# Four layers in 128 slots on one core: another timetable for the side work

## The chip, the cores and the metric

The kernel runs on one core of a Trainium2 chip. Its five engines work side by side, each through its own queue in order: PE (TensorE, matrix products and transposes), DVE (VectorE), ACT (ScalarE), POOL (GpSimd), and SP (SyncE), which here only issues DMAs. They wait for each other by semaphores. SBUF is the on-chip memory, PSUM the memory into which PE writes. The metric is the time of one execution on the device, in microseconds; a kernel's time is the median of its runs.

## The reference

An input x of 16 sequences, 512 tokens, 256 features goes through two layers, each an attention-like part and a feed-forward part, with a layer norm ahead and a residual around each. All of it is float32.

```python
x = x + _L0_attn_ref(_layernorm(x), ...)   # 16 heads, scores squared and masked, no softmax
x = x + _L0_ffn_ref(_layernorm(x), ...)    # silu(gate) * up, int8 weights, 768 hidden
x = x + _L1_attn_ref(_layernorm(x), ...)   # Mamba, forward and backward, 512 channels, 16 states
x = x + _L1_ffn_ref(_layernorm(x), ...)    # the same form, inputs and weights rounded to fp4 blocks

def step(h, ins):                          # the Mamba recurrence, over 512 tokens
    dt_t, u_t, B_t, C_t = ins
    h = jnp.exp(dt_t[..., None] * A) * h + (dt_t * u_t)[..., None] * B_t[:, None, :]
    y_t = jnp.einsum('bdn,bn->bd', h, C_t)
    return (h, y_t)
```

## The kernel before

The Mamba recurrence is the backbone. For one sequence (a block, b) there are 2 directions x 16 states x 4 groups of 128 channels = 128 scans over 512 tokens. Each is a **slot**, j = 0 to 127, and every engine walks through the slots of a block and then through the next block; the loop body holds one whole block. In slot j the fixed work is:

- POOL: for even slots the product B x (dt u) for two groups of slot j+4 (inflow, L786, 128x1024); in every fourth slot the sum of the last two token tiles (add_last, L797).
- ACT: the decay exp(dt A) of slot j+2 into one of three PSUM banks (decay, L1017), and in half of the slots the weighing of a transposed state by C (weigh_last, L1025).
- DVE: scan j (L1296), and in half of the slots the sum of a weighed state into y (add_state, L1307).
- PE: the transposes of a finished state, six slots behind (turn_state, L1598, four per slot).
- SP: in every fourth slot the row of B for the state seven slots on.

Everything else, the **side work**, is put between these: the other three layers and the rest of Mamba, of the same sequence or of the one before or after. It is cut into pieces with names: a_ is the first layer's attention (a_score the scores, with ACT's squares; a_mask POOL's mask, L732; a_weigh and a_sums the weighting of the values and the division; a_onturn and a_wo the output), f_ its feed-forward, p_ and m_ the input side of Mamba (p_in projection, p_conv convolution, p_silu, p_x, p_dt the step sizes), z_in the gate, i_turn, d_turn, d_gate and d_out the output side, q_ the fp4 feed-forward (q_gate, q_silu, q_up; q_hquant and q_htail the rounding). Five layer norms per block are split into x_stat (moments on DVE, then a root on ACT, L843 to L845), x_norm on DVE (four instructions on 128x4 elements, L1137, L1139, L1141, L1143) and the scaling on ACT (L851); x is a, f, m (twice: norm2, norm3) and q. m_x (L760) is a residual on POOL behind the scaling of norm2.

A table of rows sets the slot of every step of every piece on every engine, an entry like 50 or 22.1. On one engine the steps of a slot come after its fixed work, in the order of these numbers, and steps with the same number in the order of the rows. The fraction only orders. PE's products of side work share three PSUM banks; which bank a step gets follows from PE's part of the table, and so does the step whose reader it waits for (take_bank). Everything else that a step waits for is named by the code and does not depend on the table. The steps of an engine wait in place: one that is early holds all behind it, the scans too.

For the sequences at the ends the loop is written out, with the steps of sequences that do not exist left out; about 240 us run before the first scan and 110 behind the last one.

## Time and profile before

| what | value |
|---|---|
| median of 3 runs | 6433.99 us |
| lowest and highest | 6428.44, 6437.33 us |
| the profiled execution | 6432.07 us, span 6430.3 us |
| DVE, POOL, PE, ACT busy | 75%, 73%, 71%, 65% of the span |
| TensorE clock granted, mean | 0.849 |
| DMA | 308.76 MB, 15% of the 16 DMA engines' time |

The profile is one execution, with each instruction's start and duration, and for the idle time ahead of one the instruction elsewhere that ended it. Block 7 of 0 to 15 is read as the example: its first scan starts at 2914.16 us, the next block's at 3299.95, 385.8 later; the blocks from 2 on lie within 3 us of that. In it slot 29 starts at 2991.54, slot 50 at 3050.56, slot 84 at 3150.13, slot 91 at 3169.78, slot 96 at 3190.07, slot 109 at 3238.71 and slot 112 at 3248.55 us, by the starts of DVE's scans.

### The profile page before, as it was taken

The numbers are of one execution on the slowest core, as the hardware profiler recorded it, in microseconds if no ns is written. First come the engines' busy times: TensorE is split into PE (matmuls) and PEld (weight loads), VectorE is DVE, ScalarE is ACT, GpSimd is POOL, SyncE is SP. The second block draws the span as 40 slices with busy tenths as digits, with TensorE's granted clock in tenths as the row PEclk, the third lists the DMA queues.
The fourth block names the chain that finished last, engine by engine and source line by source line (L and its number), as shares of the span: only waits on it lengthen the run. The fifth ranks groups of instructions, "written<-read, shape, count | busy, mean of one in ns | idle before, by whom it ended". The sixth has DMA issues, their size and how long they took to land.

```text
span 6430.3 us, 79973 instructions
## 1 busy us (share of the span) xinstructions
PE 4560.3 (71%) x21853; PEld 2957.7 (46%) x21900; DVE 4819.5 (75%) x6052; ACT 4188.8 (65%) x7079; POOL 4676.2 (73%) x2442
## 2 busy tenths in 40 slices
PE   6676677777777777677777777777677777777565
PEld 4344454444445444354444445444354444445443
DVE  5477786877878787786877878787786877868774
ACT  4566666666666666666666666666666666666563
POOL 1477777778776777777778776777777778776884
PEclk9787888888888888888888888888888888888777
DMA  3111111111111111111111111111111111111110
GB/s 118 38 43 45 43 55 37 57 44 39 60 37 57 39 58 45 43 54 38 57 44 39 60 37 57 39 58 45 43 57 31 60 44 40 60 37 52 35 47 29
DMA packets 152789, 308.76 MB, mean 48 GB/s; under 512 B 20870, under 2 KB 58310, under 8 KB 149926
## 3 DMA queue, kind: packets, MB, share of 16 engines
q1 hardware_dynamic: 152278, 302.80, 15.2%
q8 instruction: 217, 3.56, 0.2%
q14 instruction: 294, 2.41, 0.1%
HBM read 285.90 MB, written 16.84 MB: 47 GB/s over the span
## 4 chain that ended last, share of the span: by engine, by line
PE 39%; ACT 19%; DVE 19%; issue 16%; POOL 6%; DVEq 1%; ACTq 0%; POOLq 0%; DMA 0%; SPq 0%
PE psum L1598 8%; DVE arena_m L1296 6%; PE psum L1411 5%; PE psum L1579 4%; ACT psum L1017 4%; ACT hc L1025 3%; POOL arena_m L786 3%; PE psum L1524 3%; PE psum L1469 3%; PE psum L1487 3%; PE psum L1452 2%; PE psum L1423 2%; DVE arena_m L1307 2%; ACT arena_a L886 2%; ACT L837 2%
## 5 line engine op out<-in xcount | busy, mean ns | idle before, releaser
L786 POOL TENSOR_TENSOR arena_m<-bS,arena_m 128x1024 f32<-128x1024 f32 x1024 | 2409.1, 2365 | 325.9 <-PE psum L1598 325.7
L1296 DVE TENSOR_TENSOR_SCAN arena_m<-psum,arena_m 128x512 f32<-128x512 f32 x2048 | 2439.8, 1209 | 105.2 <-ACT psum L1017 51.1
L1598 PE MATMUL psum<-ident,arena_m 128*128 128x128 f32 x8192 | 1477.7, 319 | 994.2 <-ACT hc L1025 690.8
L1598 PEld LDWEIGHTS psum<-ident,arena_m 128*128 128x128 f32 x8192 | 1133.7, 165 | 1615.1 <-issue 814.6
L1017 ACT ACTIVATE psum<-arena_m,Aneg 128x512 f32<-128x512 f32 x2048 | 1406.2, 693 | 573.7 <-DVE arena_m L1296 569.6
L797 POOL TENSOR_TENSOR arena_m<-arena_m,hc 128x1024 f32<-128x1024 f32 x512 | 1217.0, 2377 | 292.2 <-ACT hc L1025 291.8
L1307 DVE SCALAR_TENSOR_TENSOR arena_m<-psum,Ct,arena_m 128x512 f32<-128x512 f32 x1024 | 754.1, 737 | 535.0 <-PE psum L1598 516.7
L1025 ACT ACTIVATE hc<-psum,Ct 128x512 f32<-128x512 f32 x1024 | 695.5, 679 | 43.3 <-PE psum L1598 43.1
L886 ACT ACTIVATE arena_a<-psum 128x512 f32<-128x512 f32 (+3 forms) x1024 | 380.8, 439 | 402.7 <-PE psum L1411 316.7
L1411 PE MATMUL psum<-arena_a 64*128 64x512 f32 (+3 forms) x2048 | 441.7, 533 | 252.8 <-ACT arena_a L886 108.7
L732 POOL TENSOR_SCALAR_AFFINE_SELECT arena_a<-arena_a 128x512 f32<-128x512 f32 x256 | 165.1, 655 | 445.5 <-ACT arena_a L886 445.5
L1487 PE MATMUL psum<-wB,arena_a 128*128 128x352 f32 x1024 | 408.4, 534 | 94.5 <-ACT arena_m L992 46.9
L1250 DVE SCALAR_TENSOR_TENSOR arena_m<-psum,convw,arena_m 128x509 f32<-128x509 f32 (+2 forms) x384 | 287.1, 748 | 168.6 <-ACT arena_m L948 159.4
L741 POOL TENSOR_TENSOR arena_a<-arena_a 128x704 f32<-128x704 f32 (+1 forms) x80 | 144.9, 1811 | 349.3 <-DVE arena_a L1084 349.3
L1411 PEld LDWEIGHTS psum<-arena_a 64*128 64x128 f32 x2048 | 192.6, 212 | 393.2 <-issue 150.8
L1452 PE MATMUL psum<-arena_a,wA 128*128 128x512 bf16 x1105 | 280.7, 399 | 83.7 <-DVE arena_a L1189 41.4
L1487 PEld LDWEIGHTS psum<-wB,arena_a 128*128 128x128 f32 x1024 | 207.9, 223 | 182.0 <-issue 90.8
L1524 PE MATMUL psum<-xnT,wU 128*128 128x512 f32 x512 | 275.4, 666 | 11.3 <-DVE arena_m L1250 8.4
L948 ACT ACTIVATE arena_m<-psum,convb,convw 128x512 f32<-128x512 f32 x128 | 99.5, 777 | 230.4 <-PE psum L1524 230.2
L1579 PE MATMUL psum<-wO,arena_m 128*128 128x256 f32 x1024 | 246.4, 387 | 4.0 <-DVE xF L1279 1.8
L1532 PE MATMUL psum<-xnT,wU 128*128 128x512 f32 x512 | 236.4, 594 | 0.0
L1357 PE MATMUL psum<-ident,arena_a 128*128 128x128 f32 x640 | 125.3, 344 | 136.8 <-ACT arena_a L851 118.6
(150 smaller groups left out, 7252.8 us busy)
## 6 DMA issues: line engine op xcount, KB each, us to landing
bS<-brow SPq DMA_DIRECT2D x512, 256.0 KB, 3.3
...
```

The source lines that it names most:

```text
L786: pool.tensor_tensor(hb[s % HBS][:, two, :], bS[:, s % 2, :].unsqueeze(1).to_broadcast([P, 2, T]), du[r][:, two, :], ALU.mult).then_inc(m_ ...
L797: pool.tensor_tensor(yT[:, 2:4, :], yT[:, 2:4, :], hc[:, s % 2, :, :], ALU.add).then_inc(m_yl.sem, 1)
L886: act.activation(asq[i][:, 2 * (j % 2) + j // 2, :], bank("a_score", None, w)[:, c:c + n], ACT.Square).then_inc(a_sq.sem, 1)
L1017: act.activation(EB[j % EBS], dt[r][:, m, :], ACT.Exp, scale=Aneg[:, r, m, n:n + 1]).then_inc(m_dA.sem, 1)
L1025: act.activation(hc[:, s % 2, i, :], HT[i], ACT.Copy, scale=Ct[:, r, 2 + i, n:n + 1]).then_inc(m_hc.sem, 1)
L1296: dve.tensor_tensor_scan(v, EB[j % EBS], v, 0.0, ALU.mult, ALU.add).then_inc(m_scan.sem, 1)
L1307: dve.scalar_tensor_tensor(yT[:, i, :], HT[i], Ct[:, r, i, n:n + 1], yT[:, i, :], ALU.mult, ALU.add).then_inc(m_y.sem, 1)
L1411: ins = pe.matmul(bank("a_score", None, w - 1 + half)[:, c:c + n], kT[rows, ht, i * P:(i + 1) * P], qm[rows, j, i * P:T], start=True, stop ...
L1487: ins = pe.matmul(bank(piece, None, w)[:, 0:FIH], xTq[:, k, i * P:(i + 1) * P], w_[:, k, c * FIH:(c + 1) * FIH], start=(k == 0), stop=(k = ...
L1524: ins = pe.matmul(bank("p_in", r, m), wU[:, k, m * P:(m + 1) * P], xnT[:, k, :], start=(k == 0), stop=(k == KD - 1))
L1579: ins = pe.matmul(bank("d_out", r, i // 2)[:, (i % 2) * D:(i % 2 + 1) * D], zs[:, m, i * P:(i + 1) * P], wO[:, m, :], start=(m == 0), stop ...
L1598: ins = pe.transpose(HT[i % 2][:, m * P:(m + 1) * P], hb[s % HBS][:, m, i * P:(i + 1) * P], ident[:, :])
```

## The change

Only the table changes: the numbers in nearly all of its rows, and the order of some rows. No operation, buffer or named wait is touched; which of the three banks a product gets, and so which reader it waits for there, is worked out anew from the new table. Its core:

```diff
-        row("a_mask", None, 1, POOL=[14, 17, 17, 19, 21, 25, 26, 26, 29, 32, 36, 37, 41, 45, 46, 46])
+        row("a_mask", None, 1, POOL=[10, 17, 17, 19, 19, 26, 28, 29, 39, 39, 40, 40, 44, 48, 48, 48])
-        row("q_norm", None, -1, ACT=[65], DVE=[50])
+        row("q_norm", None, -1, ACT=[67], DVE=[29])
...
-        row("m_x", None, 1, POOL=[86])
+        row("m_x", None, 1, POOL=[89])
...
-        row("p_silu", 0, 1, ACT=[107])
+        row("p_silu", 0, 1, ACT=[108])
```

Other entries that matter below, before and after: m_norm2 on DVE 86 and 87; m_norm3 on ACT 94 and 91.4; f_norm on DVE 59 and 58, its root on ACT 58 and 58; a_sums 3 on DVE 50 and 52; a_onturn on PE 52 and 53, on ACT 52.1, 52.2 and 52, 52; p_dt of direction 1 on POOL 39, 39, 43, 53 and 40, 43, 47, 52; d_out of direction 0 on PE 75, 77, 81, 81 and 74, 76, 77, 78; the first q_gate on PE 87 and 89; p_in of direction 0 on PE from 96 and from 95; the last q_gate on ACT 108 and 110 and q_silu 3 there 108 and 110, with q_up 6 on DVE in 109 both times; p_x on PE 107, 108 and 108, 108; a_v on DVE 121, 127 and 126, 127; l_d0 on SP 75 and 55, l_Z of direction 0 28 and 45.2.

On DVE, in the pass of the loop, where slots 29 to 31 stand (L1296 is a scan, L1307 a sum into y; the four others are q_norm):

```order
 L1307 SCALAR_TENSOR_TENSOR arena_m<-psum,Ct,arena_m 128x512
-L1296 SCALAR_TENSOR_TENSOR arena_m<-psum,arena_m 128x512 x3
+L1296 SCALAR_TENSOR_TENSOR arena_m<-psum,arena_m 128x512
+L1137 SCALAR_TENSOR_TENSOR lnv<-mv 128x4
+L1139 TENSOR_TENSOR lnv<-lnv,ve 128x4
+L1141 SCALAR_TENSOR_TENSOR ve<-lnv,mv 128x4
+L1143 SCALAR_TENSOR_TENSOR shift<-mv,ve 128x4
+L1296 SCALAR_TENSOR_TENSOR arena_m<-psum,arena_m 128x512 x2
 L1307 SCALAR_TENSOR_TENSOR arena_m<-psum,Ct,arena_m 128x512
```

Three scans in a row now have the four steps behind the first of them. The same four are gone from slot 50, where they stood between a scan and the division of a_sums 3.

On ACT, slots 108 to 110 (L837 closes p_silu, L962 is the copy of p_x, L924 that of the last q_gate, L928 q_silu 3 with the load of its table, L1017 a decay, L1025 a weighing):

```order
 L837 ACT_TABLE_LOAD
 L1017 ACTIVATE psum<-arena_m,Aneg 128x512
+L962 COPY xd<-psum 128x512
+L1017 ACTIVATE psum<-arena_m,Aneg 128x512
+L1025 ACTIVATE hc<-psum,Ct 128x512
 L924 COPY arena_a<-psum 128x352
 L928 ACT_TABLE_LOAD
...
 L837 ACT_TABLE_LOAD
 L1017 ACTIVATE psum<-arena_m,Aneg 128x512
-L962 COPY xd<-psum 128x512
```

The copy of p_x stood behind q_silu 3 and now stands ahead of it, with one decay and one weighing between.

On POOL, slots 84 to 89 (L786 is an inflow, L797 an add_last, L760 is m_x):

```order
 L786 TENSOR_TENSOR arena_m<-bS,arena_m 128x1024 x2
 L797 TENSOR_TENSOR arena_m<-arena_m,hc 128x1024
-L786 TENSOR_TENSOR arena_m<-bS,arena_m 128x1024
 L760 TENSOR_TENSOR xL<-xA,arena_a 128x1024
```

m_x, which came behind the inflow of slot 86, now comes behind the add_last of slot 88.

## Rows read from the trace of the kernel before

**Rows 1.** The page: the span, then busy time of each engine, share and instructions.
```profile
span 6430.3 us, 79973 instructions
...
PE 4560.3 (71%) x21853; PEld 2957.7 (46%) x21900; DVE 4819.5 (75%) x6052; ACT 4188.8 (65%) x7079; POOL 4676.2 (73%) x2442
```

**Rows 2.** Windows: start:end, length, then busy of PE, PEld, DVE, ACT, POOL; clock; DMA.
```profile
2914.00:3300.00 386.00, 279.14 (x1358) 181.85 (x1360) 299.12 (x373) 260.64 (x441) 292.02 (x153) 0.86 0.16 48
2977.00:3007.00 30.00, 23.03 (x124) 13.37 (x124) 18.17 (x29) 23.25 (x44) 14.15 (x10) 0.80 0.05 12
3007.00:3050.00 43.00, 30.57 (x175) 17.09 (x172) 26.74 (x32) 35.71 (x73) 42.53 (x28) 0.92 0.09 26
3050.00:3061.00 11.00, 6.91 (x54) 3.36 (x52) 10.86 (x10) 4.75 (x8) 11.00 (x7) 0.98 0.42 133
3138.00:3163.00 25.00, 25.00 (x122) 18.97 (x120) 16.53 (x30) 10.57 (x21) 10.45 (x5) 1.00 0.25 90
3163.00:3190.00 27.00, 12.78 (x46) 8.29 (x44) 25.96 (x34) 20.35 (x31) 16.18 (x7) 0.69 0.29 85
3249.00:3300.00 51.00, 35.77 (x153) 24.23 (x152) 40.09 (x48) 38.73 (x71) 47.08 (x27) 0.86 0.17 50
```

**Rows 3.** The line of the scans: ns shortest/median/longest, first and last start in us.
```profile
L1296 DVE TENSOR_TENSOR_SCAN arena_m<-psum,arena_m x2048: 1159/1211/1226, 239.9 to 6319.3; 128x512 f32<-128x512 f32 x187
```

**Rows 4.** Waits of DVE in one block: who for whom, us in total, times, longest.
```profile
DVE arena_m L1307 <- PE psum L1598: 31.3, 25, 3.7
...
DVE arena_m L1296 <- POOL arena_m L786: 1.6, 2, 1.0
```

**Rows 5.** Timeline (start, us, what, idle before): q_norm on DVE, and POOL beside it.
```profile
3051.68 1.44 DVE L1137 SCALAR_TENSOR_TENSOR lnv<-mv 128x4 f32<-128x4 f32 x1
...
3053.15 2.28 DVE L1139 TENSOR_TENSOR lnv<-lnv,ve 128x4 f32<-128x4 f32 x1
...
3057.77 2.26 DVE L1143 SCALAR_TENSOR_TENSOR shift<-mv,ve 128x4 f32<-128x4 f32 x1
...
3055.36 4.66 POOL L786 TENSOR_TENSOR arena_m<-bS,arena_m 128x1024 f32<-128x1024 f32 x2
```

**Rows 6.** Timeline: first step of m_norm2 on DVE in slot 86, and POOL's m_x.
```profile
3160.40 0.16 DVE L1137 SCALAR_TENSOR_TENSOR lnv<-mv 128x4 f32<-128x4 f32 x1 [1.21 <-ACT mv L845]
...
3165.20 2.34 POOL L760 TENSOR_TENSOR xL<-xA,arena_a 128x1024 f32<-128x1024 f32 x1 [10.23 <-ACT arena_a L851]
```

**Rows 7.** Timeline: POOL's mask 8, and two waits of DVE in slots 32 and 33.
```profile
3004.05 0.64 POOL L732 TENSOR_SCALAR_AFFINE_SELECT arena_a<-arena_a 128x512 f32<-128x512 f32 x1 [7.17 <-ACT arena_a L886]
...
3001.02 0.75 DVE L1307 SCALAR_TENSOR_TENSOR arena_m<-psum,Ct,arena_m 128x512 f32<-128x512 f32 x1 [2.47 <-PE psum L1598]
...
3005.91 0.26 DVE L1163 RECIPROCAL rz<-psum 128x16 f32<-128x16 f32 x1 [3.01 <-PE psum L1431]
```

**Rows 8.** Timeline: DVE in slot 84, its wait for PE.
```profile
3154.42 0.75 DVE L1307 SCALAR_TENSOR_TENSOR arena_m<-psum,Ct,arena_m 128x512 f32<-128x512 f32 x1 [3.08 <-PE psum L1598]
```

**Rows 9.** Timeline: last of the four steps of m_norm3 on DVE, slot 91.
```profile
3176.82 2.27 DVE L1143 SCALAR_TENSOR_TENSOR shift<-mv,ve 128x4 f32<-128x4 f32 x1
```

**Rows 10.** Timeline: p_conv on DVE in slot 97, its wait for p_in.
```profile
3195.89 2.32 DVE L1250 SCALAR_TENSOR_TENSOR arena_m<-psum,convw,arena_m 128x509 f32<-128x509 f32 x3 [2.39 <-ACT arena_m L948]
```

**Rows 11.** Timeline: slots 107 to 109: ACT, then q_up 6 on DVE, then p_x on PE.
```profile
3239.79 0.69 ACT L1017 ACTIVATE psum<-arena_m,Aneg 128x512 f32<-128x512 f32 x1
3240.42 0.45 ACT L924 COPY arena_a<-psum 128x352 f32<-128x352 f32 x1
3240.88 1.28 ACT L928 ACT_TABLE_LOAD   x1
3242.18 0.79 ACT L928 ACTIVATE arena_a<-arena_a 128x704 f32<-128x704 f32 x1
...
3243.00 0.52 DVE L1227 TENSOR_TENSOR arena_a<-psum,arena_a 128x352 f32<-128x352 f32 x1 [3.08 <-ACT arena_a L928]
...
3240.79 1.88 PE L1541 MATMUL psum<-arena_m,wO 128*128 128x512 f32 x4
```

144 lines of the change are left out of this document (72 added, 72 removed).

## The prediction

> **What bounds the kernel now.** I read the page first for the shares of the engines [rows 1]. No engine is full: DVE 75%, POOL 73%, PE 71%, ACT 65%. Then the stretches of one block of 386 us in the middle of the run, by windows [rows 2]. The reader should see that DVE works 299.12 us of that block and idles 87, while POOL works 292.02, PE 279.14 and ACT 260.64. The scans (L1296) run from 239.9 to 6319.3 us, 2048 of them [rows 3], so 2.97 us each and 380 us per block, the short first one included. About 240 us before the first scan and 110 after the last are a chain without scans. So the time is 16 blocks, and a block is what DVE works plus what DVE idles. DVE takes every scan in order, ACT may be two scans ahead and POOL four, so whatever makes one engine stand reaches the others within a few slots. I therefore read which wait ends DVE's idle time [rows 4]: 31.3 us of it come before L1307, for PE's transposed state; POOL's product ends only 1.6 us. So PE and ACT being late with side work is the common case, POOL being late is rare, and each place has to be read by itself.
>
> The second thing to see is that DVE's work is not fixed. The four instructions of a normalisation (L1137 to L1143, 128x4 elements each) take 1.44 us and then three times 2.26 to 2.28 us in slot 50, 8.3 us together, while POOL runs one 2.3 us instruction after another beside them [rows 5]. The same four take 0.16 us each in slot 86, where POOL stands idle 10.23 us before L760 [rows 6]. The ends of DVE's slow ones fall on the ends of POOL's instructions. So such a chain costs 0.65 us where POOL stands, and up to 8.3 us where POOL is full. The Trainium skill (page "SBUF — State Buffer", section "Who interferes with whom") says that a DVE instruction with two SBUF inputs contends with a GpSimd instruction that reads SBUF, and that whichever comes second blocks fully. By that rule, the trace agrees: 0.16 against 2.28 us. The rule speaks against part of this change, see the second rival.
>
> **The change, part by part** (us per block; minus is faster). Nothing is added or removed: 373 DVE instructions per block stay 373. What counts is where each stands.
>
> 1. *q_norm leaves slot 50.* From 3050 to 3061 DVE is busy 10.86 of 11 us and POOL 11.00 [rows 2]; the chain is 8.3 of it [rows 5]. What is late next there: POOL, which was behind and catches up during the chain; and the end of attention (a_sums, a_onturn), which the change puts two slots later, ACT's a_onturn now in a slot before PE's. I charge 1 for those: **-7.3** (bounds -8.3 and 0, the latter if POOL, full from 3007 to 3061 [rows 2], sets the pace).
>
> 2. *q_norm arrives in slot 29.* From 2977 to 3007 POOL is busy 14.15 of 30 us, 47% [rows 2], so the chain should cost 0.65 + 0.47 x (8.3 - 0.65) = 4.3, and the wait for ACT's root right in front of it (now one slot, before 22) 1.2, the wait that m_norm2 has for its own [rows 6]: 5.5. Just behind it DVE now idles 2.47 and 3.01 us because PE's queue is behind [rows 7]; a pause of DVE lets PE catch up. I let 4 of these 5.5 be absorbed: **+1.5** (bounds -3.6 and +9.5: POOL still, 0.65 + 1.2, and 5.5 absorbed; or POOL full, 8.3 + 1.2, and nothing absorbed).
>
> 3. *The masks.* POOL stands 7.17 us in front of mask 8 because ACT's squares come later in their own queue [rows 7]; after that it is full. The change puts mask 8 ten slots behind (29 to 39), where the squares are long done, and moves two softplus sums from slot 39 to 40 and 43. But only 1.6 us of DVE's idle per block are POOL's [rows 4]: **-1** (bounds -5 and 0). Mask 4 goes the other way (21 to 19, two slots ahead of its squares); POOL idles there anyway.
>
> 4. *PE in slots 80 to 87.* PE is busy 25.00 of 25 us between 3138 and 3163 [rows 2], and DVE's longest wait there, before L1307, is 3.08 us and for PE [rows 8]. The change takes the second half of d_out out of this stretch into the eight slots before it, and a q_gate into those behind. I take two thirds of the wait, **-2** (bounds -3.1, and +2 if the slots before it become PE's bound instead).
>
> 5. *m_norm2 and m_x.* In slot 86 the chain is short only because POOL stands before L760 [rows 6]. L760 goes to slot 89, behind two products and one sum (3 x 2.35 = 7.1 us), and the chain to slot 87, so POOL may be running beside it. I take +2.5, the price of one POOL instruction (bounds 0 and +7.7). In turn POOL no longer has 10.23 us to catch up while DVE is in m_norm3, whose chain ends with 2.27 us for L1143, POOL's price again [rows 9]: -1.5 (bounds -6.8, the chain at 0.65 in place of 7.4, and 0). m_norm3 and z_in now stand in the same slot as what they wait for: +1.5. DVE is busy 25.96 of 27 here [rows 2], so nothing hides these: **+2.5**.
>
> 6. *p_in in slots 95 to 97.* DVE waits 2.39 us for ACT's p_in, which waits for PE's in its own slot [rows 10]; PE's now stands a slot ahead of it: **-2** (bounds -2.4 and 0).
>
> 7. *q_silu 3 against q_up 6.* ACT's silu (L928) ends at 3242.97 and DVE starts q_up 0.03 later after 3.08 us of idle [rows 11]. Before, the silu stands in slot 108 and q_up in slot 109. Now the silu stands in slot 110, behind the p_x copy (L962), which waits for PE's second pair of products, 3240.79 plus 1.88 [rows 11]. From its end at 3242.67: the p_x copy, a decay and a weighing, at the 0.69 of a decay each, the q_gate copy 0.45, the table 1.28 and the silu 0.79, 4.6 in all, so 3247.3. That is 4.3 later; p_silu in front may come 1 sooner, since its copy of q_gate no longer waits: **+3** (bounds +1 and +6).
>
> 8. *The rest.* f_norm goes into the slot of its own root, +1.3 (the 1.21 wait of [rows 6] is what that costs). In slots 112 to 127 POOL is busy 47.08 of 51 us [rows 2]; there DVE's wait for a_v goes away, but POOL sets the pace, so 0. Some eighty other steps move by one or two slots, some nearer to what they wait for, some farther: 0, with 3 either way.
>
> Sum: -7.3 + 1.5 - 1 - 2 + 2.5 - 2 + 3 + 1.3 = **-4.0 us per block**, 16 blocks -64 us. The profiled execution took 6432.07 us with a span of 6430.3; what lies around the scans is left as it is. 6432 - 64 = **6368 us**. The median of the three runs is 6434, 2 us above the profiled one, so the ratio is 0.990.
>
> SP's DMAs: most weights are issued 2 to 21 slots earlier (l_d0 from 75 to 55, l_Z, l_X, l_d1), three later (l_Z in slot 45, in the slot of its first product; l_g1; l_O in 126). SP stands about seven slots ahead of DVE, since it fetches the row of B for the state seven slots on, so a load in its user's slot is still issued some 20 us before it (7 x 2.97). What is new is that SP waits for PE before l_d0, behind which the next row of B is queued, and behind that POOL. No idle time of note ends on a DMA before the change; I charge nothing, within the 3 of the rest.
>
> **The rivals.**
>
> *More than that.* The late stretch of slots 20 to 50 unwinds as a whole: DVE idles 12 of 30 us from 2977 to 3007 and 16 of 43 in the next stretch. If POOL, freed of the 7.17, and ACT, with its squares a slot sooner, both keep pace, term 3 goes to its lower bound (4 lower) and term 2 to +0.5 (1 lower): -4.0 - 4 - 1 = -9, 6432 - 144 = 6288. For it: POOL, PE and ACT all have idle time there. Against: PE is the one waited for, and its work is not moved.
>
> *Slower, by POOL beside DVE's short chains.* One mechanism: a chain costs 8.3 us instead of 0.65 as soon as POOL runs back to back beside it. If the wait that kept POOL still at slot 86 is gone, m_norm2 costs +7.7 instead of +2.5; and if POOL, freed at the masks, is full in slot 29 too, q_norm costs 8.3 + 1.2 there less 4 absorbed, +5.5 instead of +1.5. -4.0 + 5.2 + 4 = +5.2, 6432 + 83 = 6515. It decides the sign from about 4 us of added overlap per block, so less than half of it is enough. For it: such chains are slow wherever POOL runs now [rows 5, 9], and POOL is busy 76% of a block [rows 2]. Against: that the chain in slot 50 is already at the full price and can only become cheaper. It is the skill's rule of the shared port (same page and section) carried to its end.
>
> *No change.* The 7.3 of term 1 are taken by the engine next in line: POOL is busy 42.53 of 43 us from 3007 to 3050 and 11.00 of 11 after that [rows 2]. If POOL sets the pace for half of the chain, slot 50 gives 3.6 and not 7.3: -0.3 per block, 6432 - 5 = 6427.
>
> **How the numbers follow.** Forecast as summed: 0.45. More: 0.15. No change: 0.18. Slower: 0.22. The bounds of the terms are worst cases (root of the squares of their halves: 11 per block); I take a third of that, 3.5 per block or 56 us, as the forecast's own error: 6312 to 6424. The range takes in the rival below and most of the one above: 6280 to 6500. A measurement here tells 0.2%, 13 us. Faster by more than that: 0.42 of the forecast, 0.15, and 0.05 of the two others: 0.62. Within: 0.02 + 0.09: 0.11. Slower: 0.27.
>
> **What would show it.** In the profile of the changed kernel: L1137 to L1143 in slot 29 with durations near 1 us and not 2.3; no idle above 1.5 us before L1307 in slots 31 to 33; POOL without the 7.17 before L732; DVE's wait before q_up 6 in slot 109 about 6 us and not 3; m_norm2's chain above 0.65; DVE's idle per block near 82 and its work 299 or less. The forecast is wrong if DVE's work per block rises above 303 (the second rival), or if POOL's idle falls under 90 with the block unchanged (the third).

## Result and the profile after the change

The changed kernel takes **6265.6 us** (median of four runs, 6262.7 to 6267.1), the kernel before 6431.2 (6425.1 to 6437.3): ratio 0.974, 95% interval 0.9725 to 0.9759. That is 166 us or 10.4 per block, where 64 and 4.0 were forecast. The sign was right and the size was not: the time lies 14 us below the low end of the range, 22 below the rival *More*. The difference isn't a general unwinding of slots 20 to 50, as that rival had it: at slot 48 the scans are 1.7 us later than before. The largest gain stands at one place that the sum had with the wrong sign, and its cause is one that the prediction had charged at nothing: where SP's queue of DMAs stands.

The page of the changed kernel, against [rows 1]:

```profile
span 6265.4 us, 79937 instructions
...
PE 4489.1 (72%) x21853; PEld 2872.4 (46%) x21900; DVE 4807.9 (77%) x6052; ACT 4183.9 (67%) x7079; POOL 4688.4 (75%) x2442
```

DVE does almost the same work, 11.6 us less in the whole run. Windows over one block and over its slots 88 to 91, columns as in [rows 2]:

```profile
2838.40:3211.60 373.20, 275.24 (x1357) 176.44 (x1360) 296.34 (x374) 259.61 (x441) 290.53 (x152) 0.87 0.15 49
...
3085.70:3094.70 9.00, 4.52 (x20) 2.59 (x20) 8.79 (x19) 6.88 (x16) 4.66 (x2) 1.00 0.33 97
```

This block is 373.2 us instead of 386. DVE works 296.3 in it (before 299.1) and idles 76.9 (before 86.9). So of the 12.8 us that this block gains, 10.0 are idle time of DVE that went away. Its waits in this block, against [rows 4]:

```profile
DVE arena_m L1307 <- PE psum L1598: 23.3, 21, 3.0
DVE arena_m L1261 <- ACT arena_m L977: 21.2, 6, 7.6
...
DVE arena_a L1227 <- ACT arena_a L928: 4.7, 2, 4.5
DVE arena_m L1296 <- POOL arena_m L786: 4.2, 3, 1.9
```

The wait for PE's state fell from 31.3 to 23.3. DVE now waits 21.2 us for ACT's p_dt (L977), 5.4 before, of which the prediction said nothing. Still the sum of the waits is 10 us smaller.

**Where in the block the gain lies.** I took the start of every scan, from the start of its own block, in blocks 3 to 12 of each profile, and subtracted the same of the kernel before. Below is this lead (minus is earlier, us per block), for the runs as well; "end" is the next block's first scan. The six other blocks gain less on average, so an end of -12.1 goes with 10.4 per block in the median. Each row is one profiled execution.

| kernel | slot 64 | 88 | 92 | 104 | end | median us |
|---|---|---|---|---|---|---|
| changed | -3.6 | -1.0 | -8.1 | -10.7 | -12.1 | 6266 |
| h_front | -4.8 | -4.8 | -4.8 | -4.9 | -5.5 | 6362 |
| h_back | +1.6 | +4.3 | -1.2 | -3.6 | -4.9 | 6373 |
| b_mx | -0.4 | -0.4 | -1.5 | -1.5 | -2.4 | 6405 |
| a_lx | -4.1 | -1.5 | -3.9 | -7.5 | -7.5 | 6329 |
| a_mx | -3.9 | -3.0 | -3.4 | -8.2 | -7.5 | 6327 |
| a_sp | -3.5 | +1.5 | -0.1 | -2.8 | -4.1 | 6375 |
| a_qnorm | -2.9 | -1.0 | -1.8 | -4.8 | -6.2 | 6328 |
| b_qnorm | -2.3 | -2.2 | -2.2 | -1.9 | -2.4 | 6393 |
| c_tail | -4.5 | -1.9 | -9.0 | -11.3 | -10.9 | 6270 |
| b_mxlx | +0.2 | +2.2 | -4.5 | -0.8 | -0.4 | 6429 |
| b_pin | +0.3 | +2.4 | -4.3 | +2.2 | +0.2 | 6433 |
| b_pin2 | -0.4 | +1.6 | -5.1 | -5.8 | -7.3 | 6333 |
| p_fn | -8.4 | -4.0 | -10.7 | -13.4 | -15.7 | 6209 |
| p_fq | -9.2 | -4.8 | -11.5 | -14.2 | -16.2 | 6201 |
| p_fqa | -10.4 | -6.0 | -12.8 | -15.5 | -4.8 | 6355 |
| p_fqa2 | -8.1 | -3.6 | -10.4 | -13.0 | -14.3 | 6227 |
| p_mix | -10.1 | -6.7 | -13.4 | -14.1 | -15.7 | 6211 |
| p_qq | -9.3 | -8.3 | -15.0 | -17.7 | -19.2 | 6161 |

In the changed kernel 7.1 us are won in the four slots 88 to 91. There stands m_norm3, term 5 of the sum. Its chain, beside those of q_norm (slot 29), m_norm2 (slot 87) and f_norm (slot 58), on DVE's timeline (start, us, instruction, idle time before), for [rows 5, 6, 9]:

```profile
2915.57 1.88 DVE L1137 SCALAR_TENSOR_TENSOR lnv<-mv 128x4 f32<-128x4 f32 x1
2917.48 2.29 DVE L1139 TENSOR_TENSOR lnv<-lnv,ve 128x4 f32<-128x4 f32 x1
2919.80 0.16 DVE L1141 SCALAR_TENSOR_TENSOR ve<-lnv,mv 128x4 f32<-128x4 f32 x1
...
3001.09 2.26 DVE L1141 SCALAR_TENSOR_TENSOR ve<-lnv,mv 128x4 f32<-128x4 f32 x1
...
3082.89 1.91 DVE L1137 SCALAR_TENSOR_TENSOR lnv<-mv 128x4 f32<-128x4 f32 x1
3084.83 0.16 DVE L1139 TENSOR_TENSOR lnv<-lnv,ve 128x4 f32<-128x4 f32 x1
...
3094.41 0.16 DVE L1141 SCALAR_TENSOR_TENSOR ve<-lnv,mv 128x4 f32<-128x4 f32 x1
3094.61 0.16 DVE L1143 SCALAR_TENSOR_TENSOR shift<-mv,ve 128x4 f32<-128x4 f32 x1
```

m_norm3's last step took 2.27 us before [rows 9] and takes 0.16 now; summed over the four steps, counted from the end of the instruction before them, and averaged over ten blocks, the chain went from 7.35 to 0.55. All averages of chains below are taken so. What lets it run is on POOL's timeline and on SP's queue:

```profile
3087.66 2.35 POOL L760 TENSOR_TENSOR xL<-xA,arena_a 128x1024 f32<-128x1024 f32 x1 [2.88 <-ACT arena_a L851]
3089.96 2.35 POOL L786 TENSOR_TENSOR arena_m<-bS,arena_m 128x1024 f32<-128x1024 f32 x1
3095.82 2.36 POOL L786 TENSOR_TENSOR arena_m<-bS,arena_m 128x1024 f32<-128x1024 f32 x1 [3.50 <-DMA bS<-brow]
```

```profile
3075.44 0.32 SPq L660 DMA_DIRECT2D wB<-kept_B  x1
3090.18 0.40 SPq L665 DMA_DIRECT2D xA<-in_L_attn_hidden_states  x1
3090.69 0.44 SPq L688 DMA_DIRECT2D bS<-brow  x1
```

POOL stands 3.50 us, from 3092.3 to 3095.8, for a row of B. The row is late because SP stood behind the load of x (L665), which the change put from slot 96 to 89 and which may not start before m_x (L760) has read the buffer, at 3090.01. The chain runs from 3094.03 to 3094.77, inside this pause. The prediction had seen that a row of B can be queued behind a waiting load, for l_d0, and had charged nothing; the load of x it did not name.

### The profile page after: what moved, and what is told of

The parts are those of the page before. It is cut to its first block and busy times, and to the rows that moved or that the text cites. A ratio compares the mean times of both kernels' runs of the same rounds, so it can differ in the third digit from the quotient of the medians.

```text
span 6265.4 us, 79937 instructions
## 1 busy us (share of the span) xinstructions
PE 4489.1 (72%) x21853; PEld 2872.4 (46%) x21900; DVE 4807.9 (77%) x6052; ACT 4183.9 (67%) x7079; POOL 4688.4 (75%) x2442
## 5 line engine op out<-in xcount | busy, mean ns | idle before, releaser
L786 POOL TENSOR_TENSOR arena_m<-bS,arena_m 128x1024 f32<-128x1024 f32 x1024 | 2429.0, 2383 | 400.6 <-PE psum L1598 349.2
L1296 DVE TENSOR_TENSOR_SCAN arena_m<-psum,arena_m 128x512 f32<-128x512 f32 x2048 | 2441.3, 1208 | 85.2 <-POOL arena_m L786 33.6
L1598 PE MATMUL psum<-ident,arena_m 128*128 128x128 f32 x8192 | 1426.2, 309 | 1020.4 <-ACT hc L1025 762.6
L1598 PEld LDWEIGHTS psum<-ident,arena_m 128*128 128x128 f32 x8192 | 1066.9, 158 | 1662.2 <-issue 889.8
L1017 ACT ACTIVATE psum<-arena_m,Aneg 128x512 f32<-128x512 f32 x2048 | 1400.2, 693 | 520.9 <-DVE arena_m L1296 508.2
L797 POOL TENSOR_TENSOR arena_m<-arena_m,hc 128x1024 f32<-128x1024 f32 x512 | 1213.6, 2370 | 307.3 <-ACT hc L1025 306.5
L1307 DVE SCALAR_TENSOR_TENSOR arena_m<-psum,Ct,arena_m 128x512 f32<-128x512 f32 x1024 | 751.8, 734 | 395.8 <-PE psum L1598 392.2
L1025 ACT ACTIVATE hc<-psum,Ct 128x512 f32<-128x512 f32 x1024 | 697.0, 681 | 62.3 <-PE psum L1598 61.5
L886 ACT ACTIVATE arena_a<-psum 128x512 f32<-128x512 f32 (+3 forms) x1024 | 386.4, 441 | 412.5 <-PE psum L1411 368.7
L1411 PE MATMUL psum<-arena_a 64*128 64x512 f32 (+3 forms) x2048 | 464.4, 559 | 190.9 <-ACT arena_a L886 78.2
L732 POOL TENSOR_SCALAR_AFFINE_SELECT arena_a<-arena_a 128x512 f32<-128x512 f32 x256 | 161.3, 645 | 328.4 <-ACT arena_a L886 328.4
L1261 DVE SCALAR_TENSOR_TENSOR arena_m<-psum,arena_m 128x512 f32<-128x512 f32 x128 | 88.0, 688 | 343.0 <-ACT arena_m L977 343.0
L1524 PE MATMUL psum<-xnT,wU 128*128 128x512 f32 x512 | 265.6, 644 | 31.3 <-DVE arena_m L1250 28.4
L1515 PE MATMUL psum<-wA,arena_a 128*128 128x256 f32 (+1 forms) x768 | 219.5, 434 | 5.5 <-ACT arena_a L939 4.1
```

The lines of the kernel that those rows point to most:

```text
L786: pool.tensor_tensor(hb[s % HBS][:, two, :], bS[:, s % 2, :].unsqueeze(1).to_broadcast([P, 2, T]), du[r][:, two, :], ALU.mult).then_inc(m_ ...
L797: pool.tensor_tensor(yT[:, 2:4, :], yT[:, 2:4, :], hc[:, s % 2, :, :], ALU.add).then_inc(m_yl.sem, 1)
L886: act.activation(asq[i][:, 2 * (j % 2) + j // 2, :], bank("a_score", None, w)[:, c:c + n], ACT.Square).then_inc(a_sq.sem, 1)
L1017: act.activation(EB[j % EBS], dt[r][:, m, :], ACT.Exp, scale=Aneg[:, r, m, n:n + 1]).then_inc(m_dA.sem, 1)
L1025: act.activation(hc[:, s % 2, i, :], HT[i], ACT.Copy, scale=Ct[:, r, 2 + i, n:n + 1]).then_inc(m_hc.sem, 1)
L1296: dve.tensor_tensor_scan(v, EB[j % EBS], v, 0.0, ALU.mult, ALU.add).then_inc(m_scan.sem, 1)
```

## Experiments

Each kernel differs from the kernel before (names in b_, h_) or from the changed one (a_, c_) by the rows shown; p_ kernels go beyond both. In the words on record "POOL's slot 92" is the place in its queue; the product made there is for the scan four slots on.

### One step of POOL: m_x

```diff
-        row("m_x", None, 1, POOL=[86])
+        row("m_x", None, 1, POOL=[89])
```

b_mx is this in the kernel before, a_mx its reverse in the changed one.

> The kernel before with one number changed: POOL's m_x (L760) stands in slot 89 instead of 86. Theory (POOL's standing moves): in the kernel before POOL stands 10.23 us in front of m_x in slot 86 and then works without a pause through slot 91, so m_norm3's chain on DVE costs 7.35 us there. With m_x in 89 POOL has done its products in time and stands during m_norm3 instead: m_norm3 from 7.35 to about 0.6, m_norm2 from 0.65 to about 2.3, so -5 us per block, 80 in all: 6351 (ratio 0.9875). Rival 1 (the recorded terms: +2.5 for m_norm2, -1.5 for m_norm3, +1 in all): 6447. Rival 2 (the cheap m_norm3 of the changed kernel comes from the moves of ACT and PE around it, z_in and m_turn, and not from m_x): m_norm3 stays near 7.3 and the time within 10 us of 6431.

> The changed kernel with POOL's m_x put back from slot 89 to 86. Theory (POOL's standing moves): m_norm3's chain goes from 0.55 back to about 7, m_norm2's from 2.3 to about 0.7, +5 us per block: 6266 + 80 = 6346. Rival 2 (the moves of z_in, m_turn and q_htail make m_norm3 cheap): both chains stay, 6266 within 10.

a_mx: 6327.2 us, 62 more than the changed kernel, and m_norm3's chain is back at 7.34 us. m_x's place is needed. b_mx: 6405.1, ratio 0.9965 (0.9952 to 0.9977): 26 us, and none of the three numbers given (6351, 6447, 6431 within 10). The chain fell only to 5.44. POOL did stand, but early, for a row of B that was late behind l_g1 in SP's slot 84, and then worked without a pause through slot 91:

```profile
3151.13 2.37 POOL L786 TENSOR_TENSOR arena_m<-bS,arena_m 128x1024 f32<-128x1024 f32 x1 [6.56 <-DMA bS<-brow]
```

So m_x's place alone does not decide. What does is when POOL stands, and here SP's queue sets that.

### The two halves

h_front has the changed kernel's rows for the steps and loads of slots 0 to 64 and the others from before; h_back is the reverse. Two loads that move from the second half into the first (l_d0 from 75 to 55, l_Z of direction 1 from 77 to 64) went with h_back.

> The rows of the changed kernel for all steps that stand in slots 0 to 64, and the rows of the kernel before for the rest. By the starts of the scans the changed kernel has won 3.4 us per block at slot 60, of 10.4 in all. Theory (the two halves add up): 6431 - 16 x 3.4 = 6376. Rival (a gain of the first half is given back later, since an engine behind it sets the pace, or the first half carries more than its slots show, since it hands the next half a queue that is less late): under 20 us of gain, or over 90.

> The rows of the changed kernel for the steps of slots 64 to 127, and the rows of the kernel before for slots 0 to 64. Theory (the halves add up): the second half wins 7.0 us per block, most of it in slots 88 to 104, so 6431 - 16 x 7.0 = 6319; m_norm3's chain near 0.6 us. Rival (halves help each other): the two gains of this run and of the front half together miss the 166 us of the whole by more than 30.

h_front: 6362.0 (ratio 0.990, 0.988 to 0.992), 69 us. h_back: 6373.0 (0.992, 0.990 to 0.994), 58 us. Together 128, and 38 short of the whole, so by my own mark (30) the halves help each other. The trace says how. In h_back m_norm3's chain takes 0.74 us from its first start to its last end in eight of ten blocks, with a mean period of 380.1 us, and 6.4 and 6.5 in two, with periods of 385.3 and 389.2. Windows of 9 us from scan 88 on in a block of each kind:

```profile
2366.90:2375.90 9.00, 4.51 (x20) 2.60 (x21) 8.84 (x19) 6.88 (x16) 4.66 (x2) 1.00 0.32 96
2745.50:2754.50 9.00, 5.91 (x12) 3.33 (x13) 7.76 (x14) 5.32 (x11) 4.65 (x2) 0.56 0.31 98
```

The granted clock is 1.00 of 2.4 GHz in all eight cheap blocks and 0.56, near the 1.2 GHz level for most of the time, in both dear ones. In the 30 us ahead PE was busy about 29 in both kinds, at 1.00. At the lower clock PE is late with its state, DVE waits before L1307, and the chain starts after POOL has gone on. Over its cheap blocks alone h_back wins 6.3 per block (380.1 against 386.4), and with h_front's 5.5 that is 11.8 of the 12.1 in the table: the halves add up where the chain is cheap. This is read from the fastest of h_back's four executions (6360.7 us; the slowest took 6384.1); how many dear blocks the others had isn't known. Why the clock falls in some blocks and not in others, I can't say from these rows.

### One DMA: the load of x

```diff
-        row("l_x", None, 2, SP=[89])
+        row("l_x", None, 2, SP=[96])
```

> The changed kernel with one DMA moved: SP's load of x (L665) back from slot 89 to 96. In the changed kernel it stands behind m_x's reading of the same buffer: SP waits until m_x ends (3090.01 us in block 7), so the rows of B behind it come late and POOL stands 3.50 us in front of L786 for slot 92, and in just this time m_norm3's chain runs on DVE in 0.65 us. Theory (the late row of B is what keeps POOL still under m_norm3): without it POOL runs its products without a pause through slot 91 and m_norm3's chain costs 4 to 7 us instead of 0.55; part comes back in q_hquant (0.89 and 2.97 in slots 94 and 95, to 0.1 and 0.9): net +3 us per block, 6266 + 48 = 6314. Rival (POOL would stand there anyway, for PE's or DVE's state, since it is four slots ahead): m_norm3 stays at 0.6 and the time within 10 us of 6266.

6329.1 us, 63 more than the changed kernel. No engine's order changed. POOL's pause is gone (first fence), and DVE's chain (second fence) waits for its instructions again:

```profile
3119.87 4.67 POOL L786 TENSOR_TENSOR arena_m<-bS,arena_m 128x1024 f32<-128x1024 f32 x2
3124.49 2.35 POOL L797 TENSOR_TENSOR arena_m<-arena_m,hc 128x1024 f32<-128x1024 f32 x1
```

```profile
3124.59 2.28 DVE L1139 TENSOR_TENSOR lnv<-lnv,ve 128x4 f32<-128x4 f32 x1
3126.90 2.26 DVE L1141 SCALAR_TENSOR_TENSOR ve<-lnv,mv 128x4 f32<-128x4 f32 x1
```

The first of them ends at 3126.87, where POOL's L797 ends (3126.84). So nothing waited for this load when it stood later, and yet the kernel is faster with it sooner, because then it holds up POOL at the right time. This one DMA carries 4.0 of the 10.4 us per block.

### All loads

a_sp is the changed kernel with every row of a load (l_) at its place in the kernel before.

> The changed kernel with all DMA loads on SP (the rows l_) at the places of the kernel before, every step of the four engines at those of the changed one. The prediction charged nothing for the loads. Theory: the load of x alone is worth 4.3 us per block (m_norm3's chain 0.55 against 5.24 us), and the other loads next to nothing; l_g1 at 84 may make a row of B late for POOL's slot 88: 6329 within 15. Rival (the loads of weights, 2 to 21 slots earlier, are worth more than that, PE waits for d_out's, f_gate's or q_down's weights): 6350 or more.

6374.6 us: 109 more than the changed kernel and 46 more than a_lx. The rival's number held, but not its reason: PE has no wait of note for a DMA in either profile. POOL's waits in the whole run, a_sp against the changed kernel (50.5):

```profile
POOL arena_m L786 <- DMA bS<-brow: 89.9, 14, 6.9
```

The row of B is now late in POOL's slot 88 (6.3 us per block), behind l_g1 in SP's slot 84, as in b_mx. POOL has that to catch up and m_norm2's chain costs 4.68 us in place of 2.31; by slot 88 the scans are 2.5 us behind the changed kernel's. m_norm3's chain then costs 4.67 in place of 0.55. These two chains are 6.5 us of the 6.8 per block that all loads together are worth, two thirds of the gain.

### The same pause in the kernel before

b_mxlx is the kernel before with m_x in slot 89, x in 89 and l_g1 in 88. b_pin adds the changed kernel's rows of m_turn, m_norm3, p_in 0 and z_silu 1; b_pin2 adds q_hturn and q_down:

```diff
+        row("m_turn", None, 1, PE=[93, 93], ACT=[93, 94])
+        row("m_norm3", None, 1, ACT=[91.4], DVE=[91])
+        row("p_in", 0, 1, PE=[95, 99.1, 101.2, 103], ACT=[96, 100.1, 102, 103])
+        row("z_silu", 1, 0, ACT=[101])
+        row("q_hturn", None, -1, PE=[98, 99, 104, 104.2, 110, 110.2, 115, 115], ACT=[98, 100, 104, 104, 111, 111, 118, 118])
+        row("q_down", None, -1, PE=[101, 105, 112, 118], DVE=[101, 107, 114, 121])
```

> The kernel before with m_x in slot 89 instead of 86, and two loads on SP moved as in the changed kernel: x (L665) from 96 to 89, the weights l_g1 (L660) from 84 to 88. With m_x alone the time was 6405 and m_norm3's chain 5.44 us, since POOL stood 6.56 us at slot 88 for a row of B behind l_g1, and ran on from there. Theory: now the row that is late is the one for slot 92, behind x, POOL stands under m_norm3, and the chain costs 0.6 instead of 5.44; 0 to 2 come back in the steps behind: -3 to -5 us per block more than m_x alone, 6325 to 6357. Rival (it takes the changed kernel's places of PE's and ACT's steps): 6405 within 10.

> The kernel before with m_x, the load of x and l_g1 as in the changed kernel (this alone made m_norm3's chain 0.55 instead of 7.35 us and left the time at 6429), and also ACT's and PE's steps just behind: m_turn from 95 to 93, m_norm3 on ACT from 94 to 91, p_in 0 from 96 to 95 on PE, z_silu 1 on ACT from 93 to 101. In the run without these DVE then waited 3.3 us for p_in in slot 97 and 2.5 for PE in slot 92, and the 6.7 us won at slot 92 were 1.6 at slot 96. Theory (two waits in a row: DVE's chain beside POOL, and PE's and ACT's steps behind it, and only both together give time): -3 us per block or more at the end, 6385 or less. Rival (what was won goes further back, to POOL in slots 112 to 127): the scans lead by 4 us or more at slot 104 and by less than 1 at the end, 6425.

> As b_pin, with q_hturn and q_down also at the changed kernel's places (ACT's second copy of q_hturn from slot 101 to 100). In b_pin ACT did z_silu of slot 101, with its table, ahead of that copy; PE waited 6.0 us in front of q_down for it and DVE 7.2 in slot 101, which undid the 5.0 us per block that the scans led by at slot 100. Theory (POOL standing under m_norm3 gives time once PE and ACT keep up behind it): the 7.2 is gone, -3 to -6 us per block at slot 104 and -2 or more at the end, 6400 or less. Rival (the rest of the kernel before takes it: another wait of the same size takes the place of each): 6425 or more.

b_mxlx: 6429.0 us, ratio 1.0004 (0.9993 to 1.0015). The chain does cost 0.55 us instead of 7.35 and the scans win 6.7 us in slots 88 to 91, but nothing of it reaches the end. My theory's time was wrong, and its mechanism only half the matter. Where it went: 2.9 of the 4.5 us that the scans led by at slot 92 are gone by slot 96, where DVE waits for PE (first line, slot 92), and 1.0 more by slot 100, where DVE comes to p_conv before ACT has p_in.

```profile
3166.78 0.75 DVE L1307 SCALAR_TENSOR_TENSOR arena_m<-psum,Ct,arena_m 128x512 f32<-128x512 f32 x1 [2.54 <-PE psum L1598]
...
3183.72 2.31 DVE L1250 SCALAR_TENSOR_TENSOR arena_m<-psum,convw,arena_m 128x509 f32<-128x509 f32 x3 [3.33 <-ACT arena_m L948]
```

b_pin: 6433.0 (1.0005), again nothing. Its lead of 5.0 us at slot 100 is lost in slot 101, where PE stands before q_down (first fence, releaser not shown). ACT, in the second fence, did z_silu with two table loads ahead of q_hturn's copies, and PE starts right behind these:

```profile
3203.34 2.05 PE L1515 MATMUL psum<-wA,arena_a 128*128 128x256 f32 x4 [6.01 <-issue]
```

```profile
3198.31 1.28 ACT L996 ACT_TABLE_LOAD   x1
3199.60 1.91 ACT L996 ACTIVATE arena_m<-arena_m 128x2048 f32<-128x2048 f32 x1
3201.53 1.28 ACT L837 ACT_TABLE_LOAD   x1
3202.82 0.27 ACT L938 COPY arena_a<-psum 128x128 f32<-128x128 f32 x1
3202.99 0.26 ACT L939 COPY arena_a<-psum 64x128 f32<-64x128 f32 x1
```

b_pin2, with these copies ahead of z_silu: **6333.1 us**, ratio 0.985 (0.983 to 0.986). That is 100 us by nine rows, where three and seven of them gave nothing (m_x alone, in b_mx, gave 26). The time won on DVE is real once the two engines behind it keep up.

### q_norm by itself

```diff
-        row("q_norm", None, -1, ACT=[67], DVE=[29])
+        row("q_norm", None, -1, ACT=[67], DVE=[50])
```

a_qnorm is this in the changed kernel; b_qnorm is the move from 50 to 29 alone in the kernel before.

> The changed kernel with q_norm's four steps on DVE put back from slot 29 to 50. By the recorded terms 1 and 2 (-7.3 and +1.5), undone: +5.8 us per block, 6266 + 93 = 6359. In the changed kernel the four take 4.4 us in slot 29 and DVE's idle time in slots 27 to 35 fell from 12.5 to 6.6. Theory A (the pause in slot 29 is taken up by that idle time): 8.0 appears in slot 50, 4.4 goes in 29 and up to 5.9 of idle time comes back: +8, 6394. Theory B (POOL, without q_norm beside it in slot 50, is now ahead there, having stood 5.2 us at slot 48): the chain costs less than 8 in slot 50, about 4: +4, 6330.

> The kernel before with q_norm's four steps on DVE moved from slot 50 to 29 and nothing else. By the recorded terms 1 and 2: -7.3 + 1.5 = -5.8 us per block, 6431 - 93 = 6338. Theory since the run with q_norm put back in the changed kernel (there f_norm's chain in slot 58 cost 0.54 us instead of 7.70 when q_norm stood in slot 50, and 7.25 in 50 took its place): a chain taken out of the full stretch hands its price to the next one. f_norm from 4.81 to about 7.7 and q_norm 4.4 in slot 29 against 8.0 in 50; -0.5 to -2.5 us per block, 6391 to 6423.

b_qnorm: 6393.1, ratio 0.994 (0.993 to 0.996), 37 us or 2.3 per block, where terms 1 and 2 had 5.8. q_norm fell from 8.02 to 4.17 us and f_norm, the next chain, rose from 4.81 to 7.33. a_qnorm: 6328.5. That is theory B's number, but not by its mechanism: q_norm costs 7.25 in slot 50, and f_norm 0.54 instead of 7.70. In all ten blocks POOL stands 5.7 to 6.0 us beside f_norm, and again for a row of B: SP held l_d0 until 3029.86 in this block, for a product of PE, and the row is queued behind it. In the changed kernel POOL comes later to this row and never waits for it. Lines of DVE and of POOL:

```profile
3034.76 0.16 DVE L1139 TENSOR_TENSOR lnv<-lnv,ve 128x4 f32<-128x4 f32 x1
...
3035.54 2.36 POOL L786 TENSOR_TENSOR arena_m<-bS,arena_m 128x1024 f32<-128x1024 f32 x1 [5.79 <-DMA bS<-brow]
```

By slot 64 a_qnorm is only 0.7 us behind the changed kernel. Its loss lies in slots 88 to 91, where it has the same rows. In seven of ten blocks the chain of m_norm3 takes 6.4 to 6.6 us (mean period 382.5), in two it takes 0.75 (375.2 and 375.4), and in one 2.9. The granted clock over these slots is 0.56 or 0.57 in all seven dear blocks and 0.81 in the other three. Windows over slots 88 to 91 in a dear and in a cheap block:

```profile
2732.50:2741.50 9.00, 5.93 (x12) 3.33 (x13) 7.76 (x14) 5.32 (x11) 4.65 (x2) 0.57 0.34 99
3114.70:3123.70 9.00, 5.21 (x16) 3.02 (x16) 8.04 (x15) 5.62 (x12) 4.66 (x2) 0.81 0.34 99
```

And the dear block on DVE, then on POOL:

```profile
2742.61 0.75 DVE L1307 SCALAR_TENSOR_TENSOR arena_m<-psum,Ct,arena_m 128x512 f32<-128x512 f32 x1 [1.88 <-PE psum L1598]
2743.28 1.64 DVE L1137 SCALAR_TENSOR_TENSOR lnv<-mv 128x4 f32<-128x4 f32 x1
2744.95 2.27 DVE L1139 TENSOR_TENSOR lnv<-lnv,ve 128x4 f32<-128x4 f32 x1
```

```profile
2742.54 2.36 POOL L786 TENSOR_TENSOR arena_m<-bS,arena_m 128x1024 f32<-128x1024 f32 x1 [3.47 <-DMA bS<-brow]
```

PE, more of the time at the lower clock, makes DVE wait 1.88 us instead of 0.77. The chain starts at 2743.28, 0.74 us after POOL has gone on, and costs 7 us of period. In the cheap block it starts 0.6 us before. In its cheap blocks a_qnorm's period is within 1.1 us of the changed kernel's mean of 374.3: apart from the dear blocks, that is all that q_norm's own move is worth beside the rest of the change. Whether its old place also causes the lower clock, and so the dear blocks, isn't shown.

### Two waits of the changed kernel taken away

```diff
-        row("q_silu", None, -1, ACT=[91.3, 97, 103, 110])
+        row("q_silu", None, -1, ACT=[91.3, 97, 103, 108])
-            DVE=[113.1, 114.2, 116, 117], POOL=[114, 114.2, 117, 117]
+            DVE=[113.1, 114.2, 116, 118], POOL=[114, 114.2, 117, 121]
```

with q_gate's last two places as they were before the change.

> The changed kernel with three waits mended that its trace shows: ACT's fourth q_silu and q_gate copies back from slots 110, 108, 110 to 108, 107, 108, PE's q_gate from 107 to 106, DVE's last p_dt from 117 to 118 and POOL's two from 117 to 121 (with 118, 121 as before the change for the last). DVE waits 4.5 us for q_silu 3 and 4.3 for p_dt 3; in the kernel before 3.06 and 0.74. Theory (these waits are on the path): -1.5 and -3 us per block, 6266 - 72 = 6194. Rival (as slots 112 to 127 showed in the kernel before, POOL sets the pace there, and takes what is won): within 20 us of 6266, with POOL's idle time in slots 112 to 127 gone.

6269.8 us: nothing. The wait of 4.50 for q_silu 3 is gone and in its place, two slots on, DVE waits for PE; the 4.28 for p_dt are gone, and a_norm's chain, now beside POOL, costs 6.1 us in place of 2.9:

```profile
3170.11 0.75 DVE L1307 SCALAR_TENSOR_TENSOR arena_m<-psum,Ct,arena_m 128x512 f32<-128x512 f32 x1 [4.72 <-PE psum L1598]
```

The rival's number held, for another reason than it gave: POOL's idle time in slots 112 to 127 only fell from 3.6 to 2.7 us, and what took the gain is PE's queue and the chain.

### Taking the price away instead of moving it

p_fn takes f_norm's chain from DVE to POOL, into POOL's odd slot 59, which has no product. It is written as six steps; r, t, q, h, v are the root, the scratch, and the results and variance of the norm. The semaphore waits between the steps are left out here.

```diff
-        row("f_norm", None, 1, ACT=[59], DVE=[58])
+        row("f_norm", None, 1, ACT=[59], POOL=[59])
+                pool.tensor_tensor(t, r, r, ALU.mult)
+                pool.tensor_tensor(t, t, v, ALU.mult)
+                pool.tensor_scalar(t, t, -0.5, 1.5, ALU.mult, ALU.add)
+                pool.tensor_tensor(q, t, r, ALU.mult)
+                pool.tensor_tensor(h, mv[:, n, :, 0], q, ALU.mult)
+                pool.tensor_scalar(h, h, -1.0, None, ALU.mult)
```

p_fq does it for q_norm too (POOL=[33]), p_fqa also for a_norm (POOL=[118]), and p_fqa2 has a_norm's at POOL=[116.5] instead.

> The changed kernel with f_norm's chain of 128x4 steps taken from DVE (slot 58) to POOL (its slot 59, two slots ahead of DVE), as six steps since POOL is given products and scalings only. On DVE the chain costs 7.70 us per block, beside a POOL that works without a pause, and DVE is busy 22.7 of 23.3 us in slots 56 to 63. Theory (the price is that of the two engines in each other's way, so it goes away with the instruction on DVE): DVE's work falls by 7.7 us per block, POOL's rises by 1 to 3; POOL's wait of 5.6 us at its slot 64 takes that up; -3 to -6 us per block, 6170 to 6218. Rival (POOL sets the pace in slots 48 to 64, and each us more on it is one more of the block): +1 to +3 per block, 6282 to 6314.

> As the run before, with q_norm (DVE slot 29 to POOL's slot 33) and a_norm (DVE 117 to POOL's 118) also on POOL: three of five chains. On DVE these cost 4.4 and 2.9 us in the changed kernel. Theory: q_norm's 4.4 were taken up by idle time, and slots 112 to 127 are paced by POOL (busy 47.8 of about 50 us there), so beyond the run with f_norm alone only 0 to 2 us per block: 6140 to 6218. Rival (each chain on DVE is on the path): another -7 per block, near 6100; rival (POOL is the next engine in line in slots 112 to 127): +1 to +3 per block against the run with f_norm alone.

> The changed kernel with f_norm's and q_norm's chains on POOL (its slots 59 and 33) and a_norm's left on DVE. With a_norm also on POOL the time was 6355, and there ACT waited 10.5 us for a_norm's chain, which stood behind six softplus sums of 1.27 us and a product on POOL, and DVE 12.4 us for PE in slot 120; up to slot 116 its scans led those of the run with f_norm alone by 1.5 to 2.5 us per block. Theory: without that place the lead stays: 6209 - 16 x 2 = 6177. Rival (q_norm's time is idle time anyway, and POOL has 1.9 us more to do): 6209 within 12.

> As p_fq, with a_norm's chain on POOL too, but ahead of the softplus sums (slot 116 instead of 118). Theory: ACT gets a_norm's scale no later than from DVE, DVE saves 2.9 us and POOL, which is the busy one in slots 112 to 127 (idle 3.6 of 50 us), does 1.9 more: +0 to +2 us per block against p_fq, 6177 to 6209. Rival (DVE's chain is what holds the end of the block): -1 to -3, down to 6130.

p_fn: **6208.8 us**, ratio to the kernel before 0.966 (0.964 to 0.968), 57 us below the changed one, inside what the theory gave. On POOL the six steps take 1.85 us with the gaps, where four cost DVE 7.7. First and last step, and ACT's wait for them:

```profile
2962.70 0.20 POOL L779 TENSOR_TENSOR lnv<-mv 128x4 f32<-128x4 f32 x1
...
2964.33 0.22 POOL L791 TENSOR_SCALAR shift<-shift 128x4 f32<-128x4 f32 x1 [0.20 <-POOL shift L788]
```

```profile
2964.59 2.08 ACT L870 ACTIVATE arena_a<-xA,shift,ve 128x256 f32<-128x256 f32 x4 [1.55 <-POOL shift L791]
```

p_fqa: 6355.0, 146 us worse than p_fn, a miss of all three numbers. Up to slot 116 it leads p_fn. Then ACT stands 10.48 us for a_norm's chain, behind six softplus sums and a product in POOL's queue, and everything behind ACT stands too:

```profile
3232.80 1.58 ACT L870 ACTIVATE arena_a<-xA,shift,ve 128x256 f32<-128x256 f32 x3 [10.48 <-POOL shift L791]
```

p_fq, without that place: 6200.7 (0.963, 0.962 to 0.965). That is 8 us below p_fn, with intervals that overlap, so here the rival held: q_norm's time was idle time anyway. p_fqa2, with a_norm ahead of the sums: 6227.4 (0.968), 27 more than p_fq. That is 1.7 per block, near the upper end of the 0 to 2 expected against p_fq, though p_fq itself was put at 6177. So a_norm doesn't pay on POOL.

### Who takes back what the chain gives

p_fn leads the changed kernel by 7.7 us at slot 60 and by 3.0 at slot 88. p_mix has the front half and the two chains on POOL of p_fq, and from slot 64 on the rows of b_pin2; between slots 64 and 84 these are those of the kernel before. p_qq is p_fq with one row changed:

```diff
-        row("q_quant", None, -1, DVE=[69, 70, 70, 70, 73, 73], POOL=[73, 74, 79])
+        row("q_quant", None, -1, DVE=[67, 68, 68, 68, 69, 71], POOL=[73, 74, 74])
```

> A kernel put together from what the runs showed: the changed kernel's rows for slots 0 to 64, f_norm's and q_norm's chains on POOL, the rows of b_pin2 for the rest (the kernel before with m_x, the load of x, l_g1, m_turn, p_in, z_silu, q_hturn and q_down moved). By the gains apart: at slot 60 the scans of p_fq lead the kernel before by 11.9 us per block; from slot 84 on b_pin2 won 6.6. Theory A (they add, and the middle rows of the kernel before cost nothing, as in h_front): -18 per block, 6143. Theory B (what f_norm's chain gives is handed back in slots 60 to 84 whichever rows stand there, since POOL and PE are not ahead any more; p_fq lost 6.3 there): -12 per block, 6240; p_fq had -15.

> As p_fq, with q_quant back at the kernel before's places (DVE 67 to 71 in place of 69 to 73, POOL's last in 74 in place of 79). In p_fq one step of q_quant costs DVE 3.4 us beside POOL and POOL then stands 7.3 us for the last of them. Theory: steps two slots sooner take POOL's wait away and some of the 6.3 us that p_fq loses in slots 60 to 84: -1 to -3 us per block, 6153 to 6185. Rival (PE sets the pace in slots 72 to 84): 6201 within 12.

p_mix: 6211.5 us (0.965). Of its lead of 10.1 at slot 64 it still has 8.8 at slot 80, where p_fq has 3.5 of 9.2: so it is the changed rows of slots 64 to 80 that take this time back, as theory A said. The total is between the two theories all the same. The back half won the 7 us that it won in b_pin2 (from -8.7 at slot 84 to -15.7), but 4.1 of the 12.8 us that p_mix led by at slot 60 were gone by slot 72. p_qq: **6160.6 us**, ratio 0.958 (0.956 to 0.959), 40 below p_fq, as its theory had it. p_fq and p_qq on POOL, first step of q_quant's tail, and p_qq's page:

```profile
3011.25 2.37 POOL L741 TENSOR_TENSOR arena_a<-arena_a 128x1024 f32<-128x1024 f32 x1 [7.32 <-DVE arena_a L1103]
```

```profile
2976.55 2.36 POOL L741 TENSOR_TENSOR arena_a<-arena_a 128x1024 f32<-128x1024 f32 x1 [0.63 <-DVE arena_a L1103]
```

```profile
span 6158.8 us, 80244 instructions
...
PE 4499.3 (73%) x21900; PEld 2882.0 (47%) x21900; DVE 4629.2 (75%) x5924; ACT 4181.2 (68%) x7079; POOL 4721.0 (77%) x2634
```

p_qq is 105 us faster than the changed kernel and 270 faster than the one before.

## Why the prediction missed, step by step

By halves the terms say -5.5 for the front (1, 2, 3 and f_norm of 8) and +1.5 for the back (4 to 7). Measured are -4.3 (h_front) and -3.6 (h_back), and 2.4 more for both together. So the front carried the right sign, and the back half's was wrong.

1. **q_norm leaves slot 50 (-7.3).** The price at the place was right: slots 48 to 55 gained 8.6 us. The step that failed is "what is late next there", charged at 1. What pays is the next chain on DVE: f_norm rose by 2.9 us and f_rest, two instructions beside POOL, by 2.2, and slots 56 to 63 gave 3.3 back. With term 2, b_qnorm measured -2.3 where -5.8 stood, and beside the rest of the change a_qnorm's cheap blocks say about -1, its whole time -3.9.
2. **q_norm arrives in slot 29 (+1.5).** The chain took 4.4 us on average (forecast 4.3). It was not near 1 us at each step, as "what would show it" said, but 1.9, 2.3, 0.16 and 0.16: a step either waits out POOL's instruction or costs 0.16, and an average busy share gives only the mean. DVE's idle time in slots 24 to 35 is 7.0 us, and 10.9 in p_fq and 11.3 in a_qnorm, which lack only this chain on DVE there. So about 4 were absorbed, as I took. The wait of 1.2 for the root did not come. The arrival cost about nothing: from slot 24 to 36 the changed kernel and a_qnorm both gain 1.1.
3. **The masks (-1).** POOL no longer waits 7.17 us at mask 8; the waits of L732 fell from 445.5 to 328.4 us in the run. What it is worth by itself wasn't tried: h_front's 4.3 less b_qnorm's 2.3 leave 2 us for all of the front half's other moves, the masks among them. One of these moves costs, and no term named it: slots 36 to 47 lost 3.7 us (the same in h_front and a_qnorm). DVE's first two steps of p_dt moved from slots 38 and 40 to 37 and 38, level with and ahead of ACT's, now in 37 and 39. DVE waits for ACT's p_dt 2.33 and 6.35 us in these slots, and in slot 46 for 7.64 (4.56 before). No run moved them back. The last of these waits:

```profile
2970.99 0.69 DVE L1261 SCALAR_TENSOR_TENSOR arena_m<-psum,arena_m 128x512 f32<-128x512 f32 x1 [7.64 <-ACT arena_m L977]
```

4. **PE in slots 80 to 87 (-2).** These slots gained 0.9, but the eight slots 72 to 79 lost 2.5 and slots 64 to 71 1.0. The bound "+2 if the slots before it become PE's bound instead" came about in size, but only half by PE: of the 2.5, 1.2 are idle time (DVE waits 1.5 and 2.0 us for PE in slots 76 and 79) and 1.4 are DVE's work, two steps of q_quant put there. In p_qq, with q_quant back, both waits for PE are still there and the loss is 1.2.
5. **m_norm2, m_x, m_norm3 (+2.5).** This is the step that failed most. m_norm2 went from 0.65 to 2.31, as charged, and its wait for the root, 1.2, went. But m_norm3 went from 7.35 to 0.55, by 6.8, the bound that I gave and set aside for -1.5. I reasoned from how much POOL has to catch up, and not from what POOL would wait for next, which was the row of B behind the load of x. Slots 84 to 87 lost 1.2 us and slots 88 to 91 gained 7.1; in place of +2.5 that is -5.9, a distance of 8.4, more than the whole miss of 6.4. The runs bear it out only for the rows as a set: with m_x or the load of x put back 3.9 and 4.0 us are lost.
6. **p_in (-2).** Slots 92 to 103 gained 2.6, and the wait of 2.39 in slot 97 is gone. Right; and b_mxlx shows more than I saw in it: without these moves term 5 gives nothing.
7. **q_silu 3 (+3).** The wait is 4.50 in place of 3.08, against the 6 expected; slots 104 to 111 lost 1.5. c_tail shows that it isn't the bound there at all: take it away and PE's queue is.
8. **The rest, and SP (0).** f_norm's wait for its root is 0.27 and not 1.3. The last sixteen slots gained 2.9. The loads, charged at nothing "within the 3 of the rest", are worth 6.8 us per block by a_sp. The list there didn't name the load of x (from 96 to 89), the one that mattered most. "No idle time of note ends on a DMA before the change" was true and proved nothing, since a queue's order can make one.

The rival of the slower kernel had the mechanism (a chain's price is POOL's state beside it) and the wrong direction, because it asked only where POOL would become full and not where it would come to stand. By the Trainium skill (page "SBUF — State Buffer", section "Who interferes with whom") whichever of the two comes second blocks fully; the trace agrees: in a_lx and a_qnorm DVE's steps of 2.27 us end with POOL's instruction, and 0.6 us before POOL's next instruction or 0.7 behind its start decide between 0.75 and 6.4.
